# A recommender ranker on one core: VectorE places the rows fetched one by one, ScalarE fetches thirteen fields in one run, layer 3 moves forward, h1 goes in quarters

## The reference

```python
x0 = emb[ids].reshape(2048, 1664)
x = x0
for i in range(3):
    x = x0 * (x @ cross_w[i])[:, None] + cross_b[i] + x
h = relu(x0 @ w1 + b1)                     # 1664 x 1024
h = relu(h @ w2 + b2)                      # 1024 x 512
h = relu(h @ w3 + b3)                      # 512 x 256
out = sigmoid(concat([x, h], axis=1) @ out_w + out_b)
```

## Time and profile before

| | |
|---|---|
| median of 3 runs | 515.7 us (515.51 to 515.76) |
| the profiled execution's own time | 515.57 us |
| its span in the trace | 513.8 us |
| PE busy | 478.8 us, 93% of the span |
| POOL busy | 372.1 us, 72% |
| DVE busy | 247.9 us, 48% |
| ACT busy (DMA issues are not counted) | 33.5 us, 7% |
| granted TensorE clock, mean | 0.992 |

### The profile page before, as it was taken

One profiled execution on the slowest core, in us unless ns is written; L12 is line 12 of the kernel. 1 busy time (PEld: TensorE's weight loads), 2 busy tenths in 40 slices (PEclk: granted clock), 3 DMA queues, 4 the chain that ended last, 5 costly groups with the idle time before them and its releaser, 6 DMA issues.

```text
span 513.8 us, 13128 instructions
## 1 busy us (share of the span) xinstructions
PE 478.8 (93%) x2912; PEld 444.7 (87%) x2912; DVE 247.9 (48%) x490; ACT 33.5 (7%) x68; POOL 372.1 (72%) x400
## 2 busy tenths in 40 slices
PE   2699899998998999899899999999999899999997
PEld 1399798898998889899799989888898889999996
DVE  5776446354363635436264443645454263544335
ACT  4642000000000000000000000000000000000112
POOL 5777777777777777777777777777777777777740
PEclk9999999999999999999899999999999899999999
DMA  7981111111111111111111111111111111111100
GB/s 223 385 300 29 29 28 26 31 27 27 29 29 28 26 32 27 28 30 27 28 28 30 28 28 30 29 26 28 29 28 26 31 28 26 28 29 26 27 18 2
DMA packets 18142, 24.61 MB, mean 48 GB/s; under 512 B 7845, under 2 KB 8832, under 8 KB 18064
## 3 DMA queue, kind: packets, MB, share of 16 engines
q0 software_dynamic: 12576, 12.90, 11.3%
q1 hardware_dynamic: 4154, 9.71, 5.3%
q10 hardware_dynamic: 1334, 1.17, 0.7%
HBM read 24.41 MB, written 0.01 MB: 48 GB/s over the span
## 4 chain that ended last, share of the span: by engine, by line
PE 61%; POOL 18%; issue 11%; DMA 6%; DVE 3%; ACT 0%; POOLq 0%; DVEq 0%
PE l_bank L733 50%; POOL x_raw L345 18%; DMA x_raw<-in_L_rec_emb,idx 6%; PE x_bank L745 4%; PE x_bank L733 2%; PE h_bank L787 2%; DVE x_raw L510 2%; PE l_bank L818 1%; PE h_bank L757 1%; DMA ids<-in_r_ids 1%; PE h_bank L829 0%; PE l_bank L757 0%; DVE xT_lo L534 0%; PE h_bank L733 0%; DVE xT_hi L517 0%
## 5 line engine op out<-in xcount | busy, mean ns | idle before, releaser
L345 POOL DMA_INDIRECT x_raw<-in_L_rec_emb,idx x393 | 371.2, 945 | 122.2 <-issue 107.6
L733 PE MATMUL l_bank<-w_hi,xT_hi 128*128 128x342 f32 (+1 forms) x624 | 144.9, 333 | 0.1
L733 PE MATMUL l_bank<-w_lo,xT_hi 128*128 128x342 f32 (+1 forms) x624 | 138.5, 322 | 0.0
L733 PE MATMUL l_bank<-w_hi,xT_lo 128*128 128x342 f32 (+1 forms) x624 | 138.1, 321 | 0.0
L733 PEld LDWEIGHTS l_bank<-w_lo,xT_hi 128*128 128x128 f32 x624 | 107.3, 191 | 0.0
L733 PEld LDWEIGHTS l_bank<-w_hi,xT_hi 128*128 128x128 f32 x624 | 105.0, 192 | 2.6 <-DVE xT_lo L534 0.4
L733 PEld LDWEIGHTS l_bank<-w_hi,xT_lo 128*128 128x128 f32 x624 | 106.9, 191 | 0.0
L517 DVE CAST xT_hi<-x_bank 128x512 fp32r<-128x512 f32 (+2 forms) x56 | 33.1, 592 | 94.2 <-PE x_bank L745 94.2
L510 DVE COPY_PREDICATED x_raw<-past,x_bank 128x512 f32<-128x512 int32 (+1 forms) x66 | 40.3, 610 | 57.4 <-DMA x_raw<-in_L_rec_emb,idx 56.9
L745 PE MATMUL x_bank<-identity,x_raw 128*128 128x128 f32 x208 | 34.8, 280 | 17.0 <-DVE x_raw L510 16.9
L733 PE MATMUL l_bank<-w_hi,h1T_hi 128*128 128x512 f32 x120 | 48.7, 406 | 0.9 <-DVE h1T_lo L539 0.9
(11 more groups left out here) (97 smaller groups left out, 310.4 us busy)
## 6 DMA issues: line engine op xcount, KB each, us to landing
ids<-in_L_rec_emb SPq DMA_DIRECT2D x1664, 0.2 KB
ids<-in_L_rec_emb ACTq DMA_DIRECT2D x1280, 0.2 KB
w_raw<-in_L_rec_w SPq DMA_DIRECT2D x18, 512.0 KB, 14.6
x_raw<-in_L_rec_emb,idx POOLq DMA_INDIRECT x393, 2.4
b_rows<-in_L_rec_b ACTq DMA_DIRECT2D x1, 512.0 KB
b_rows<-in_L_rec_b ACTq DMA_DIRECT2D x1, 256.0 KB
ids<-in_r_ids SPq DMA_DIRECT2D x1, 208.0 KB, 2.6
b_rows<-in_L_rec_b ACTq DMA_DIRECT2D x1, 128.0 KB
```

What stands on the lines that cost most here:

```text
L345: pool.indirect_dma_start(out=dst, out_offset=None, in_=emb, in_offset=rows).then_inc(landed, 16)
L733: done = pe.matmul(bank[:, 0:b - a], x[:, k, :], w[:, k, a:b], start=(k == 0 and n == 0), stop=(k == last_k and n == 2))
```

## The change

ACT's list of tiles grows from ten to thirteen (2, 12 and 15 are new), so POOL has three gathers less. ACT fetches 16 rows ahead of its last hi copy of tile 0, 16 behind it, and then all the rest in blocks of 32, with nothing in between but the wait for a free buffer. DVE places the rows of SP and of ACT, in front of `make_whole` of the group that needs them. The hi copies of tile 15's groups 0 and 1 and of h2 of tile 14 go from ACT to DVE; those of groups 2 to 5 stay on ACT, behind all its fetching. Layer 3 of tile t-1 goes from the end of step t to in front of the transposes of x group 2, and has a bank of its own (`h_bank[1]`); `l3_out` goes behind group 2's copies on DVE. h1 is transposed and copied in four quarters over four banks in all tiles, and the transposes wait for `h3_ready` of tile t-1; its hi copies of tile 0 are DVE's too, and `dots_out` goes behind h1's copies. The last step's h1 was in quarters already.

```diff
-    ACT_TILES = [3, 4, 5, 6, 8, 9, 10, 11, 13, 14]
+    ACT_TILES = [2, 3, 4, 5, 6, 8, 9, 10, 11, 12, 13, 14, 15]
-    ACT_SHARES = [24, 28, 24, 28]
-    assert all(sum(ACT_SHARES) * (t - 1) >= P * (j + 1) for j, t in enumerate(ACT_TILES))
+    ACT_FIRST = 16
+    ACT_REGS = 32
...
-        l3_bank = [x_bank[0]] * (TILES - 1) + [h_bank[1]]
+        l3_bank = h_bank[1]
-        H1_LAST = [h_bank[0], x_bank[0], h_bank[1], x_bank[1]]
+        H1_BANK = [h_bank[0], x_bank[0], h_bank[1], x_bank[1]]
...
             def first_step():                                  # ACT
...
+                    if g == NG - 1:
+                        act.wait_ge(sp_idx_ready, 1)
+                        fetch(ACT_FIRST)
                     x_hi(0, g)
-                h1_hi(0)
-
-            def step(t):
-                if t in SP_TILES or t in ACT_TILES:
-                    act.wait_ge(x_transposed, NG * t + 1)
-                if t in SP_TILES:
-                    sp_place(t)
-                if t in ACT_TILES:
-                    act_place(t)
-                for share in ACT_SHARES:
-                    fetch(share)
+                fetch(ACT_REGS - ACT_FIRST)
+                while fetched[0] < P * len(ACT_TILES):
+                    fetch(ACT_REGS)
 
             def last_step(t):
-                x_hi(t, 0)
-                h2_hi(t - 1)
-                for g in range(1, len(LAST_GROUPS)):
+                for g in range(2, len(LAST_GROUPS)):
                     x_hi(t, g)
...
+            def place(t, g):                                   # DVE
+                if t in SP_TILES and SP_FIELD // FPK in groups(t)[g]:
+                    i = SP_TILES.index(t)
+                    dve.wait_ge(sp_landed[i % SP_BUFS], 16 * P * (i // SP_BUFS + 1))
+                    dve.tensor_copy(x_buf[t % 2][:, SP_FIELD * E:(SP_FIELD + 1) * E], sp_rows[i % SP_BUFS]).then_inc(sp_placed, 1)
+                if t in ACT_TILES and ACT_FIELD // FPK in groups(t)[g]:
+                    j = ACT_TILES.index(t)
+                    dve.wait_ge(act_landed[j % ACT_BUFS], 16 * P * (j // ACT_BUFS + 1))
+                    dve.tensor_copy(x_buf[t % 2][:, ACT_FIELD * E:(ACT_FIELD + 1) * E], act_rows[j % ACT_BUFS]).then_inc(act_placed, 1)
+
             def make_whole(t, g):
+                place(t, g)
...
             def h1_lo(t):
-                for half in range(2):
-                    if t > 0:
-                        h1_hi(t, half)
-                    dve.wait_ge(h1T_hi_ready, 2 * t + half + 1)
+                for q in range(QUARTERS):
+                    h1_hi(t, q)
+                    dve.wait_ge(h1T_hi_ready, QUARTERS * t + q + 1)
...
             def step(t):                                       # DVE
...
+                    if g == 2:
+                        l3_out(t - 1)
                 l1_out(t)
+                h1_lo(t)
                 dots_out(t)
-                h1_lo(t)
-                l3_out(t - 1)
...
             def l2(t, ks):                                     # PE
-                pe.wait_ge(h1T_ready, 2 * t + 1 + ks[-1] // HB)
...
                 for k in ks:
+                    if k % QB == 0:
+                        pe.wait_ge(h1T_ready, QUARTERS * t + k // QB + 1)
...
             def step(t):                                       # PE
                 begin(t)
                 for g in range(1, NG):
                     l1(t, g, slice(0, -ahead(t)))
+                    if g == 1:
+                        l3(t - 1)
                     if g < NG - 1:
                         transpose_x(t, g + 1)
                     l1(t, g, slice(-ahead(t), None))
                 transpose_h1(t)
-                l3(t - 1)
```

More of the change, by code:

```diff
@@ L50, in dcn_ranker_kernel @@
     SP_BUFS = 4
-    ACT_TILES = [3, 4, 5, 6, 8, 9, 10, 11, 13, 14]
+    ACT_TILES = [2, 3, 4, 5, 6, 8, 9, 10, 11, 12, 13, 14, 15]
     ACT_FIELD = GROUPS[2][-1] * FPK
     ACT_BUFS = 2
-    ACT_SHARES = [24, 28, 24, 28]
-    assert all(sum(ACT_SHARES) * (t - 1) >= P * (j + 1) for j, t in enumerate(ACT_TILES))
-    ONE_RUNS = [(SP_FIELD, range(2, TILES - 1)), (ACT_FIELD, range(3, 7)), (ACT_FIELD, range(8, 12)), (ACT_FIELD, range(13, 15))]
+    ACT_FIRST = 16
+    ACT_REGS = 32
+    ONE_RUNS = [(SP_FIELD, range(2, TILES - 1)), (ACT_FIELD, range(2, 7)), (ACT_FIELD, range(8, 16))]
     AT_ROWS = [(f, t) for f, tiles in ONE_RUNS for t in tiles]
@@ L182, in dcn_ranker_kernel @@
         h_bank = [pb(f"h_bank{i}") for i in range(2)]
-        l3_bank = [x_bank[0]] * (TILES - 1) + [h_bank[1]]
-        H1_LAST = [h_bank[0], x_bank[0], h_bank[1], x_bank[1]]
-        QB = K2 // len(H1_LAST)
+        l3_bank = h_bank[1]
+        H1_BANK = [h_bank[0], x_bank[0], h_bank[1], x_bank[1]]
+        QUARTERS = len(H1_BANK)
+        QB = K2 // QUARTERS
+        assert HB % QB == 0
         NH = N2 // 2
@@ L394, in fetch @@
                     share -= rows
[L396 to L400, removed]
             def x_hi(t, g):
@@ L406, in x_hi @@
                                x_bank[g % 2][:, 0:len(ks) * P], ACT.Copy).then_inc(xT_hi_ready, 1)
-            def h1_hi(t):
-                for half in range(2):
[L410 to L417, removed]
             def h2_hi_last(t):
@@ L425, in h1_hi_last @@
             def h1_hi_last(t):
-                for q, bank in enumerate(H1_LAST):
-                    act.wait_ge(h1_transposed, 2 * t + q + 1)
+                for q, bank in enumerate(H1_BANK):
+                    act.wait_ge(h1_transposed, QUARTERS * t + q + 1)
                     act.activation(h1T_hi[:, q * QB:(q + 1) * QB, :].rearrange("p k b -> p (k b)"),
@@ L468, in _ @@
             first_step()
-            act.wait_ge(sp_idx_ready, 1)
-            for t in range(1, TILES - 1):
-                step(t)
             last_step(TILES - 1)
@@ L521, in relu_hi, with h1_hi @@
                 dve.tensor_scalar(hi, bank[:, 0:cols], 0.0, None, ALU.max).then_inc(done, 1)
-            def h1_hi(t, half):
-                dve.wait_ge(h1_transposed, 2 * t + half + 1)
-                relu_hi(h_bank[half], HB * P, h1T_hi[:, half * HB:(half + 1) * HB, :].rearrange("p k b -> p (k b)"), h1T_hi_ready)
+            def h1_hi(t, q):
+                dve.wait_ge(h1_transposed, QUARTERS * t + q + 1)
+                relu_hi(H1_BANK[q], QB * P, h1T_hi[:, q * QB:(q + 1) * QB, :].rearrange("p k b -> p (k b)"), h1T_hi_ready)
             def h2_hi(t):
@@ L578, in h1_lo @@
             def h1_lo(t):
-                for half in range(2):
-                    if t > 0:
-                        h1_hi(t, half)
-                    dve.wait_ge(h1T_hi_ready, 2 * t + half + 1)
-                    part = slice(half * HB, (half + 1) * HB)
-                    relu_lo(h_bank[half], HB * P, h1T_hi[:, part, :].rearrange("p k b -> p (k b)"),
+                for q in range(QUARTERS):
+                    h1_hi(t, q)
+                    dve.wait_ge(h1T_hi_ready, QUARTERS * t + q + 1)
+                    part = slice(q * QB, (q + 1) * QB)
+                    relu_lo(H1_BANK[q], QB * P, h1T_hi[:, part, :].rearrange("p k b -> p (k b)"),
                             h1T_lo[:, part, :].rearrange("p k b -> p (k b)"), h1T_ready)
             def h1_lo_last(t):
-                for q, bank in enumerate(H1_LAST):
-                    dve.wait_ge(h1T_hi_ready, 2 * t + q + 1)
+                for q, bank in enumerate(H1_BANK):
+                    dve.wait_ge(h1T_hi_ready, QUARTERS * t + q + 1)
                     part = slice(q * QB, (q + 1) * QB)
@@ L793, in transpose_h1 @@
                     pe.wait_ge(h2T_ready, t)
-                for half in range(2):
-                    h1_chunks(t, h_bank[half], range(half * HB, (half + 1) * HB))
+                    pe.wait_ge(h3_ready, t)
+                for q, bank in enumerate(H1_BANK):
+                    h1_chunks(t, bank, range(q * QB, (q + 1) * QB))
             def transpose_h1_last(t):
                 pe.wait_ge(h3_ready, t)
-                for q, bank in enumerate(H1_LAST):
+                for q, bank in enumerate(H1_BANK):
                     h1_chunks(t, bank, range(q * QB, (q + 1) * QB))
             def l2(t, ks):
-                pe.wait_ge(h1T_ready, 2 * t + 1 + ks[-1] // HB)
                 if t == 0:
@@ L843, in l3 @@
                 for k in ks:
-                    done = three_passes([(l3_bank[t], 0, N3)], h2T_hi, h2T_lo, w3_hi, w3_lo, k, K3 - 1)
+                    done = three_passes([(l3_bank, 0, N3)], h2T_hi, h2T_lo, w3_hi, w3_lo, k, K3 - 1)
                 if k == K3 - 1:
```

20 lines of the change are left out of this document (7 added, 13 removed).

## The result

The changed kernel takes 538.0 us (median; 536.51 to 538.43), the kernel before 515.7: a ratio of 1.0428, 95% interval 1.0407 to 1.0449. It is slower by 22.3 us. The profiled execution took 537.77 us, with a span of 536.0.

A forecast was written before the change was run, and what follows sets the result against it. It took ACT's stream of row fetches to become the bound: 51.0 + 464 + 1.0 to layer 1 + 21.7 of tail + 1.5 for the clock + 1.8 from span to device time = 541.0, rounded down to 540 us, range 526 to 546.

The forecast's parts named there:

- Start: ACT's first 32 rows, 16 ahead of tile 0's last hi copy and 16 behind it, are out at 51.0 us.
- Blocks: ACT's remaining fetches: 51 blocks of 32 rows at 9.1 us each, 464 us, with the last issue at 515 us.
- End: From ACT's last issue through hi copies and DVE's subtraction to layer 1 of tile 15's chunks 7 and 8: 1.0 us.
- The clock: In tile 15's layer 1, a granted clock lowered by PE's longer wait adds 1.5 us.
- The 21.7 us of tail: From the start of layer 1 of tile 15's chunks 7 and 8 to the span's end, left unchanged.
- The 9.1: Cost in us of one ACT block of 32 rows: 31 issues of 0.217 plus a load's gap of 2.36.
- The 1.9 us from a field's last issue to its transposes: Per tile: 0.9 for landing, 0.22 for DVE's placing copy, 0.87 for make_whole and its hand-over.
- The due times: ACT's fields against group 2's transposes: tiles 2 to 4 in time, 5 level, 6 late by 8 us, 12 onward late.
- Part 4: h1 in quarters: PE waits 0.3 us at layer 2 and 0.5 at group 0, step 29.5 us, costed at nothing.
- Part 3: Layer 3's 12 matmuls, 1.42 us, move in front of group 2's transposes: costs nothing in sum.
- Part 2: DVE places rows: two copies of 0.22 us a tile in front of group 2, hidden or within the 1.9 us.
- The rival in which ACT keeps up: Blocks of at most 8.5 us let ACT finish in time: a span of 510.7, time 512.5 us; chance 9%.

The follow-up runs named there:

- run 1: The changed kernel with the ten ACT tiles of the kernel before in place of thirteen: 515.84 us, 1.0006 of the kernel before.
- run 3: The changed kernel, thirteen fields, with 16 registers a load in place of 32: 559.7 us, 1.0861 of the kernel before.
- run 5: The changed kernel with twelve fields for ACT, all tiles from 2 to 15 but 6 and 11: 514.76 us, 0.9984 of the kernel before.
- run 6: The changed kernel with twelve fields for ACT, all tiles from 2 to 15 but 6 and 7: 515.66 us, 1.0002 of the kernel before.
- run 2: The kernel before with only layer 3 forward and h1 in quarters; ACT places and fetches ten fields by the old shares: 515.78 us, 1.0007.
- run 7: The changed kernel with ten fields and four more SBUF-to-SBUF copies a tile on DVE, into a spare tile: 516.84 us, 1.0026 of the kernel before.
- run 9: Run 5 with make_whole of the next tile's group 0 on DVE between h1's second and third quarter: 514.82 us, 0.9977 of the kernel before.
- run 4: The changed kernel with tile 15's remaining hi copies of x on DVE in place of ACT: 533.6 us, 1.0347 of the kernel before.

## Why the prediction was right

**The bound.** Forecast 540 (526 to 546), measured 538.0. ACT's stream is the bound: run 1 shows it by the number of rows, run 3 by the cost of a block, runs 5 and 6 by the due times. The mechanism held, and the sum came out 3 us high before rounding.

**The terms.** Start: 51.0 us for the first 32 rows, 51.3 in the trace. Blocks: 51 x 9.1 = 464 us forecast, 51 x 9.00 = 459.1 measured, 5 us less and the largest miss. The load's gap for 32 registers was put at 2.36 and is 2.43 on the mean; the issues were put 0.217 us apart and are 0.212. A small part of that is the long issue behind each load (run 3): there are fewer loads a row now, and the prediction had spread these issues evenly over the rows. The rest is small differences and rounding. End: 1.0 us to layer 1 was put and 1.8 measured (510.40 to 512.18), for `make_whole` and the transpose of chunk 12 stand in front of it, which the prediction left out. The clock was put at 1.5 and cost 2.15 us in those 18 matmuls. The 21.7 us of tail were right. So the stream was 5 us too long in the forecast and the end 1.4 too short: in part the two misses cancel, and that is luck.

The 9.1 rests on a condition that the prediction doesn't name: it came from rows of ACT of which one in eight moves, and so do the rows of the changed kernel. The 1.9 us from a field's last issue to its transposes don't hold for each field either. Where the last rows of a field are past the table, its placing begins 0.08 to 0.09 us behind the last issue (tiles 12, 13 and 14), and not 0.9; for tile 6 it was 0.99.

**The due times.** Tile 6 was forecast 8 us late, at 226, and came at 225.74. Tile 5 was level and waited 1.8. Some 6 us were forecast at each of the tiles 12 to 14: tile 13 waited 6.63, but tile 12 only 0.46, and for POOL, and tile 14 only 1.92. Tiles 12 to 15 have their fields out at 402.1, 439.0, 474.2 and 510.4, 3 to 5 us ahead of my list. Behind tile 13's wait the granted clock was 0.5 up to 445.2, and PE was busy 32.9 us up to tile 14's transposes where run 1 had 30.5: a slower PE took up what would have been waiting.

**Part 4.** A stall of 0.3 us at layer 2 was forecast, 0.24 measured. One of 0.5 at group 0 was forecast, and 0.10 to 0.12 measured. A step of 29.5 was forecast, 29.26 measured. **Part 3** was put at nothing in sum, and runs 1 and 2 agree (0.9997 to 1.0016 of before). **Part 2** was put at nothing; runs 1 and 2 agree, and by run 7 (a quarter of its 1.0 us) its copies cost some 0.3 us, an estimate. The rival in which ACT keeps up was priced at 512.5 us; run 5, where ACT does keep up with one field less, takes 514.8. The price took PE's last wait for POOL to be at tile 14, at 457.6. In run 5 it is at tile 13, at 428.93, and PE's own work brings tile 14 only at 459.78: fewer gathers on POOL gain nothing more once PE is bound.

Not tried: loads of more than 32 registers, SP's faster issue for the thirteen fields, and ids that all lie in the table.

## What to carry to other kernels

A queue that issues DMAs is as much an engine as the one that computes, though the busy column leaves it out: before giving it more, multiply its own cost a row (loads included) by the rows, and set each piece against its due time. Here a stream that looked 5% busy was full, and the thirteenth field cost 23 us where the eleventh and twelfth together had gained 1. Take the cost of a row with the data it will run on: here seven of eight DMAs move nothing. When one engine sets the pace, longer steps elsewhere are free only until the last tiles, where the pace-setter is done and they are paid.

## What the runs showed of the hardware

- ACT issues a DMA of one row from a register every 0.18 us when the bounds check leaves the row out (issue 0.09 us). One that moves its 256 bytes takes 0.24, and the first such behind a register load 0.47. A load of 32 registers leaves a gap of 2.41 us in the median, one of 16 a gap of 1.43. With every row in the table a block of 32 would take some 4 us more (an estimate: 28 more rows, 0.15 us more for each).
- SP does 32 rows in 427.69 / 52 = 8.2 us beside ACT's 9.0 in the same run.
- Copies of VectorE from SBUF to SBUF in fp32 and GpSimd's gathers disturb each other little (run 7): of 37 gathers beside a copy 8 took 1.02 to 1.08 us in place of 0.94.
- After a wait of TensorE of 2.2 us the granted clock was at half (1.2 of 2.4 GHz) for 3.4 us in run 9, and in the changed kernel for 10.2 us around the wait of 7.7 us. Behind run 4's wait of 2.65 us, at 513.17, it stayed at 2.4 GHz, so the length of a wait alone doesn't tell. By stretches of the changed kernel (us; PE, PEld, DVE, ACT, POOL; granted clock):

```profile
510.05:516.88 6.83, 5.14 (x19) 5.18 (x20) 1.47 (x5) 0.66 (x2) 0.00 (x0) 0.50 0.00 1
219.92:230.16 10.24, 4.42 (x17) 4.45 (x18) 3.42 (x8) 0.00 (x0) 5.47 (x6) 0.50 0.11 21
```

Its price is small as long as something else is waited for anyway, as at tile 14, and whole in the tail: at 510 it cost 2.15 us of the 22.
